# A second looped slot of one-hots in a graph kernel's matrix build, with the looped source one-hots made on ScalarE

## The reference

```
neigh = segment_sum(h1[src], dst, num_segments=N)              # layer 0
msg   = where(edge_type == 0, msgs[0], msgs[1]); agg = segment_sum(msg, row)   # layer 1, twice
agg   = segment_sum(h[src], dst); z = (1 + e) * h + agg        # layer 2, five times
out   = segment_sum(support[src] * edge_vals[:, None], dst)    # layer 3
```

## Time and profile before

| | us |
|---|---|
| median of three runs | 1826.44 |
| lowest and highest | 1819.98, 1828.72 |
| the profiled execution | 1818.69 |
| its span | 1816.4 |
| the build in it | about 20 to 316 |

### The profile page before, as it was taken

The page is one execution under the profiler, slowest core; times in us unless marked ns, Lnnn a source line. Parts: engine busy times, 40 slices in busy tenths (PEclk is TensorE's granted clock), DMA queues, the critical chain, the costliest instruction groups (busy, mean ns, idle before and its releaser), DMA issues.

```text
span 1816.4 us, 22290 instructions
## 1 busy us (share of the span) xinstructions
PE 1754.4 (97%) x7318; PEld 849.3 (47%) x7318; DVE 874.3 (48%) x1889; ACT 593.8 (33%) x1232; POOL 10.8 (1%) x36
## 2 busy tenths in 40 slices
PE   5989888999999999999999999999999999999998
PEld 3555555433334444444444444444544444444444
DVE  7888887489885321112222224334253443594123
ACT  1555544466876311222110001232323323232000
POOL 1000000000000000000000000000000000000000
PEclk9999999999999999999999999999999999999999
DMA  7999989810302401000011116300000010021111
GB/s 176 247 288 280 247 235 245 318 36 2 144 24 82 168 4 43 0 1 23 0 47 35 35 35 241 147 0 30 1 0 30 1 41 1 1 82 58 35 47 47
DMA packets 45781, 157.80 MB, mean 87 GB/s; under 512 B 7686, under 2 KB 9630, under 8 KB 37094
## 3 DMA queue, kind: packets, MB, share of 16 engines
q1 hardware_dynamic: 43792, 146.95, 26.6%
q10 hardware_dynamic: 1878, 9.44, 1.4%
HBM read 120.71 MB, written 35.65 MB: 86 GB/s over the span
## 4 chain that ended last, share of the span: by engine, by line
PE 83%; DVE 6%; DMA 5%; issue 3%; DVEq 2%; ACT 1%; POOL 0%; POOLq 0%; ACTq 0%
PE psum L1549 31%; PE psum L1563 31%; PE psum L1790 7%; DMA hs<-in_L_gnn_basis 4%; PE psum L1477 2%; PE psum L1444 2%; PE psum L1740 2%; PE psum L1637 2%; PE psum L1624 1%; PE psum L1476 1%; PE psum L1515 1%; DMA adj<-in_L_gnn_basis 1%; DVE hs L716 1%; DVEq L695 1%; PE psum L1716 1%
## 5 line engine op out<-in xcount | busy, mean ns | idle before, releaser
L1563 PE MATMUL psum<-hs,adj 128*128 128x512 f16 x2880 | 636.3, 380 | 0.0
L1549 PE MATMUL psum<-wb,xt 128*128 128x512 f32 x1056 | 457.7, 593 | 0.0
L1563 PEld LDWEIGHTS psum<-hs,adj 128*128 128x128 f16 x2880 | 281.2, 98 | 330.6 <-issue 11.0
L1549 PEld LDWEIGHTS psum<-wb,xt 128*128 128x128 f32 x1056 | 199.2, 190 | 244.8 <-issue 243.2
L1328 ACT ACTIVATE ua<-ua 128x512 f32<-128x512 f32 x60 | 37.8, 629 | 314.9 <-DVE ua L1106 181.2
L1102 DVE SCALAR_TENSOR_TENSOR vt<-psum,scl,xt 128x512 f32<-128x512 f32 x60 | 44.8, 746 | 192.7 <-PE psum L1563 192.7
L1037 DVE TENSOR_TENSOR vt<-psum,adj 128x512 f32<-128x512 f32 x24 | 16.6, 692 | 249.0 <-PE psum L1549 249.0
L1549 PE MATMUL psum<-adj,xt 128*128 128x512 f32 x288 | 130.1, 595 | 0.0
L1790 PE MATMUL psum<-hs,adj 128*128 128x512 f32 (+1 forms) x312 | 123.8, 560 | 0.0
L1477 PE MATMUL psum<-hs 128*128 128x192 f32 x404 | 99.7, 329 | 0.0
L1316 ACT ACTIVATE lnst<-lnst,bcol 128x1 f32<-128x1 f32 x24 | 7.1, 295 | 280.1 <-DVE lnst L1015 270.6
(11 more groups left out here) (249 smaller groups left out, 1741.5 us busy)
## 6 DMA issues: line engine op xcount, KB each, us to landing
hs<-in_L_gnn_basis SPq DMA_DIRECT2D x38, 960.0 KB, 12.9
adj<-in_L_gnn_basis SPq DMA_DIRECT2D x26, 960.0 KB, 14.5
aw_scratch<-xt ACTq DMA_DIRECT2D x12, 768.0 KB, 10.4
adj<-aw_scratch SPq DMA_DIRECT2D x1, 9216.0 KB, 36.8
x_scratch<-adj SPq DMA_DIRECT2D x24, 256.0 KB, 2.3
hs<-x_scratch SPq DMA_DIRECT2D x24, 256.0 KB, 2.6
ts_scratch<-adj SPq DMA_DIRECT2D x2, 2304.0 KB, 19.0
as_scratch<-adj SPq DMA_DIRECT2D x1, 4608.0 KB, 16.8
```

What stands on the lines that cost most here:

```text
L1549: x = pe.matmul(psum[:, bank, :], xt[:, i, k, :], w[:, k, :], start=first and k == 0, stop=last and k == 3)
L1563: x = pe.matmul(psum[:, i % 2 + (4 * half if own else 0), :], adj[:, m, j, P * i:P * i + P], hs[:, t, half, j, :], start=n == 1 or (own an ...
```

## The change

There are two looped slots, used by even and odd windows. The source one-hot of a looped tile is no longer made by VectorE but by ScalarE, in two instructions: `Abs(key - column)` into a scratch array `apart_t`, then `Relu(1 - that)` into the slot. ScalarE does this in `sources(w + 2)`, which stands at the end of its iteration of window w, behind the evictions and lots; `sources(0)` and `sources(1)` run ahead of the loop. For each looped tile of window w + 2 it waits until the slot is free, so a second looped tile of a window waits until TensorE has counted that window's first. TensorE waits for `onehot_ready` of the slot (VectorE's keys) and for the new `source_ready`. The running sum over the steps is made twice, over even and over odd windows, since each slot has counts of its own.

```
-SLOTS = 5
+SLOTS = 6
+        looped_t = sb("looped", [P, P + W * NT + W * NT], F32)
...
+        apart_t = rest[:, N + 256 + 2 * SLOT:N + 512 + 2 * SLOT].rearrange("p (t x) -> p t x", t=2)
+        onehots_at = [pairs[0][:, 0, :], ..., pairs[1][:, 1, :], looped, looped_t[:, :]]
-        LOOPED = SLOTS - 1
+        def looped_slot(w):
+            return 4 + w % 2
...
-            step(dve.tensor_tensor_scan(wrow[0:1, 2, :], wrow[0:1, 1, :], wrow[0:1, 1, :], 0.0, ALU.add, ALU.bypass))
+            by_turn = wrow[0:1, :, :].rearrange("p a (w t) -> p a t w", t=2)
+            for t in range(2):
+                x = dve.tensor_tensor_scan(by_turn[:, 2, t, :], by_turn[:, 1, t, :], by_turn[:, 1, t, :], 0.0, ALU.add, ALU.bypass)
+            step(x)
...
                 with dve.Fori(0, steps) as q:
-                    dve.wait_ge(onehot_free[LOOPED], before + q + 1)
+                    dve.wait_ge(onehot_free[looped_slot(w)], before + q + 1)
                     last = nc.s_assert_within(first + q + 2, 0, EC - 1, skip_runtime_bounds_check_because=why)
-                    source(LOOPED, last)
-                    keys(LOOPED, last, n, u)
+                    keys(looped_slot(w), last, n, u)
...
+            def sources(w):
+                first, steps, before = unpack(act.value_load(wrow_i[0:1, 0, w:w + 1], min_val=0, max_val=PACKED))
+                apart = apart_t[:, w % 2, :]
+                with act.Fori(0, steps) as q:
+                    t = nc.s_assert_within(first + q + 2, 0, EC - 1, skip_runtime_bounds_check_because="a tile of this stretch")
+                    act.wait_ge(onehot_free[looped_slot(w)], before + q + 1)
+                    act.activation(apart, iota_s[:, 0:P], ACT.Abs, bias=ecol[:, 0, bass.ds(t, 1)], scale=-1.0).then_inc(apart_ready[w % 2], 1)
+                    act.wait_ge(apart_ready[w % 2], before + q + 1)
+                    act.activation(onehot_s[looped_slot(w)], apart, ACT.Relu, bias=1.0, scale=-1.0).then_inc(source_ready[w % 2], 1)
+            act.wait_ge(c_ready, 7)
+            sources(0)
+            sources(1)
...
-                act.wait_ge(onehot_free[LOOPED], through + 1)
+                act.wait_ge(onehot_free[looped_slot(w)], through + 1)
...
                 for lot in by_window[w]:
                     side_lot(*lot)
+                if w + 2 < NW:
+                    sources(w + 2)
...
                 with pe.Fori(0, steps) as q:
-                    pe.wait_ge(onehot_ready[LOOPED], before + q + 1)
-                    counts(b, LOOPED, False)
+                    pe.wait_ge(onehot_ready[looped_slot(w)], before + q + 1)
+                    pe.wait_ge(source_ready[w % 2], before + q + 1)
+                    counts(b, looped_slot(w), False)
```

More of the change, by code:

```diff
@@ L209, in program @@
         pairs.append(rest[:, N + 256:N + 256 + 2 * SLOT].rearrange("p (k x) -> p k x", k=2))
-        onehots_at = [pairs[0][:, 0, :], pairs[0][:, 1, :], pairs[1][:, 0, :], pairs[1][:, 1, :], looped]
+        apart_t = rest[:, N + 256 + 2 * SLOT:N + 512 + 2 * SLOT].rearrange("p (t x) -> p t x", t=2)
+        onehots_at = [pairs[0][:, 0, :], pairs[0][:, 1, :], pairs[1][:, 0, :], pairs[1][:, 1, :], looped, looped_t[:, :]]
         onehot_s = [v[:, 0:P] for v in onehots_at]
@@ L238, in program @@
         onehot_free = [sem(f"onehot_free{k}") for k in range(SLOTS)]
+        apart_ready, source_ready = [[sem(f"{what}{t}") for t in range(2)] for what in ("apart_ready", "source_ready")]
         krel_ready = sem("krel_ready")
@@ L707, in sources @@
                                   ecol[:, 0, bass.ds(t, 2)].unsqueeze(2).broadcast_to([P, 2, P]), ALU.is_equal)
-            def source(k, t):
-                dve.tensor_scalar(onehot_s[k], iota_s[:, 0:P], ecol[:, 0, bass.ds(t, 1)], None, ALU.is_equal)
             def keys(k, t, n, u):
```

## The result

The change makes the kernel slower. The median is 1846.08 us (1844.25 to 1848.44, four runs) against 1823.21 us for the kernel before on the same chip (1814.05 to 1828.72, four runs): a ratio of 1.0132 [1.0112, 1.0152], some 24 us (the medians themselves lie 22.9 apart). The profiled execution after took 1848.44 us, against 1818.69 of the one before, so the two profiles lie 30 us apart, which is more than the medians do; single executions of the kernel before spread over 15 us.

The account below looks back on a forecast made before the run. The prediction took the build as paced by its transfers, TensorE and VectorE close behind. Terms -2 + 0.2 + 1 + 7 + 3 = 9.2, taken as 10 us, gave 1836 us against the median 1826.4; 8-in-10 range 1812 to 1862.

Parts of the forecast that it names:

- VectorE's source goes: Build: VectorE loses 30.3 us of busy time; taken as 0 in the middle, 2 us gained at the start.
- The pair: ScalarE, each of 106 looped tiles: Abs 384 ns and Relu 310 ns, together 0.69 us, unable to overlap.
- A window's extra: ScalarE, per window: pair plus exposed register work, 0.69 + 0.55 = 1.25 us, bounds 0.69 and 1.6.
- The ten waits: ScalarE at ten windows with two looped tiles: idle about 1.5 us each, bounds 0 and 2.8; 12 us in the middle.
- The sum of the middle: ScalarE, 47.5 to 262.3: 209.6 us of work plus 12 of waits, 221.6, 7 us over 214.8.
- The last stretch: Build from 262.3 on: two more waits each delay a chunk's reissue about 1.5 us, 3 us in all.
- TensorE's waits for its semaphore: TensorE, each looped tile: one more semaphore, 51 ns, 5.4 us if exposed, taken as hidden under matmuls: 0.
- the chain ahead of the build: Ahead of the build: one more running sum, under 0.35 us, overlapping the first, taken as 0.2 us.
- ScalarE far behind: Rival, middle: register work exposed in full, 1.6 us a window, 34 us over, 6 more at the ends: 1866; chance 0.08.
- VectorE was the brake: Rival, build: transfers have room, VectorE's keys hold TensorE; about -17 us, 1809; chance 0.17.
- The transfers keep the pace: Rival, build: ScalarE fits in, change does nothing that shows, between -8 and +4 us: 1824; chance 0.25.
- The rule weighed on the transfers: Basis chunk loads: by the 358 GB/s limit a chunk needs some 2.9 us; set aside for the trace's 216 GB/s.

Follow-up runs that it names:

- m_lean_wait: e_lean with all sources made two windows ahead again, so the ten waits are back; 1825.60 us, 1.0011 of the kernel before.
- i_one_load: Changed kernel with one ScalarE register load a window less, eviction's count kept from the value loaded for `sources`, ten waits kept; 1827.4 us, 1.0018 of before.
- c_free_source: Changed kernel in which nobody makes the looped tiles' sources, slots zeroed once, counts of looped tiles left out; 1817.9 us, 0.9965 of before.
- b_two_slots: Changed kernel with the looped sources back on VectorE, so the kernel before with a second looped slot alone; 1823.18 us, 0.9996 of before.
- e_lean: a_kept without the second register load a window on ScalarE, nothing else changed; 1822.8 us, 1.0009 of the kernel before.
- d_before_half: Kernel before with 60 of 120 partitions of every basis chunk loaded and used; 1822.2 us, 0.9993 of the kernel before.
- d_free_half: c_free_source with 60 of 120 partitions of every basis chunk loaded and used; 1809.1 us, 0.9931 of the kernel before.
- a_kept: Changed kernel with only the first looped tile's source made two windows ahead, later ones just ahead of their own window's eviction; 1843.84 us, 1.0110 of before.
- f_single: Changed kernel without the Abs and its register work, one Relu of the column numbers making each looped source; 1821.7 us, 0.9998 of before.
- h_one_ahead: Changed kernel with the sources made one window ahead in place of two; 1883.10 us, 1.0344 of the kernel before.

## Why the prediction was right, and where its sizes failed

The direction, the place and the mechanism were as forecast, and the time lies in the range; the size was not: 10 us forecast, 24 by the ratio and 30 between the profiles. Luck had two parts in it. The prediction named the wrong brake for the kernel before; that did no harm, as it charged ScalarE's work against the measured length of the middle, whatever set it. And its direction hung on the waits: ScalarE's work alone, 209.6 us, still fitted into 214.8. Measured, the work alone is already 217.2 (162.0 + 55.2), and m_lean_wait and i_one_load show that waits of the same size cost next to nothing where it is less. Point by point:

- **VectorE's source goes, 0 in the middle, 2 us at the start.** Nearly right by c_free_source (6 us in all), for a reason that was half wrong. The prediction had the transfers as the pace; halving them brought 1 us, some 6 with all of the clock's part allowed for. Its gain of 2 us at the start did not come: 22.0 us against 21.5.
- **The pair, 0.69 us.** 0.714 by the rows; right, no table load on top.
- **A window's extra, X = 1.25.** The first step that failed. In the middle ScalarE has 51.1 us more busy time and 55.2 us of issue gaps, which makes (51.1 + 55.2) / 79 = 1.35. Its parts are 0.65 for the pair (51.1 / 79; the two overlap their neighbours a little), 0.50 behind the Relu (39.7 / 79, forecast 0.55), and 0.20 ahead of the Abs (15.5 / 79), where the forecast took 0 as "hidden by the lot in front". It isn't hidden behind the DMA issue of L1181, which stood in the code and which the sum passed over: that write comes nine times in the middle, and at the six of them that an Abs follows at once, ScalarE stands 1.43 to 1.48 us, 8.7 of the 15.5 us. The other 6.8 us lie in 13 gaps of 0.4 to 0.7 us. The term was too small by 0.1 x 79, 7.5 us.
- **The ten waits, 1.5 us each.** 22.1 us in ten, 2.2 each; 17.4 in the middle where 12 was forecast: 5 us. Their places were right; the longest took 3.5, over the bound of 2.8.
- **The sum of the middle.** 221.6 forecast, 240.3 measured, 18.7 missing: 7.5 and 5.4 from the two terms above, 3.5 of small waits (2.1 + 1.4) and 2.2 that stand in no row. None of these is large. They count in full because the forecast's ScalarE already stood 7 us over the stretch: past that edge an error of 0.1 us a window is paid 79 times. i_one_load shows it from the other side, 21 us for one load a window.
- **The last stretch, +3.** Measured 56.7 against 53.7: +3.0.
- **TensorE's waits for its semaphore, the chain ahead of the build, the start.** The first eviction comes 0.2 us later and the start is 0.5 us longer, where 1.2 was forecast for chain and table load. b_two_slots has the longer chain and loses nothing; TensorE's added semaphore wait was not tried alone.
- **The clock** was taken as full throughout. It wasn't (below); TensorE is busy 5.7 us longer for the same matmuls. The profiled execution before, with 1.000, is not typical of its kernel either, which has 0.998 in the mean.

Of the rivals, "ScalarE far behind" (X = 1.6, 1866) had the better picture of what was to come, ScalarE past the edge, and too high an X. "VectorE was the brake" falls by c_free_source and by i_one_load and e_lean: where ScalarE keeps up the time is that of before, not 17 us less. "The transfers keep the pace" has the right time for the lean versions, 1823 to 1827; the runs don't bear out its reason.

The signs that were named came: L1214's wait for TensorE 9.9 us (under 50), ten waits before the Abs, TensorE waiting for ScalarE's turn copies, VectorE's busy time down (238.3 to 218.0 us in the build, 20 rather than 30), the DMA share at 0.91 in the middle. Of the two signs of being wrong, the pair with its register work under 1 us a window did not come (1.35). The other, chunk issues closer than 4.5 us, can't tell: they are 2.6 to 14.2 us apart before already, and on average 5.2 after instead of 4.68.

The rule weighed on the transfers (the Trainium skill, DMA: Bandwidth & Descriptors, section Bandwidth, about 358 GB/s) was set aside because "nowhere in the build is the traffic at that level, 261 GB/s with everything in it". That reading was wrong: 261 is a mean over 215 us, and the same trace has 350 GB/s over 10 us and 405 over 3 us in the build, all traffic taken together (shown at d_before_half). The kernel after has such a stretch too, 356 GB/s in 288.3 to 291.3 (last section). So the 216 GB/s of the earlier trace rows were what was asked for in that stretch, and not the most that the transfers can do, and d_before_half says the same. The rival that the prediction tied to the rule and calls the third is "VectorE was the brake", the second in its list. The rule's premise, transfers with time to spare, is borne out; the gain of 17 us is not, as even with sources that cost nobody anything (c_free_source) only 6 us came.

**What stays open.** The clock's exact part of the 24 us: a kernel with the same gaps but full clock was not tried. The mean granted clocks, 0.9960 after against 0.9980 to 0.9986 before, bound it by an estimate: (0.0020 to 0.0026) x 1846, 4 to 5 us at most. Whether i_one_load (1.0018) and m_lean_wait (1.0011), which keep the ten waits, still lose a little against e_lean (1.0009), which doesn't, is within their intervals. And that two brakes share the build before rests on d_free_half, whose interval allows a plain sum too, and on d_before_half, which was disturbed by its clock.

## What to carry to other kernels

Slack that an engine shows as one large wait (137 us here) is to be charged with everything that its queue has to run, in order: instructions, register loads, loop ends, DMA issues, and waits in front of work that others need. When the sum comes near the length of the stretch, the price per item turns from nothing to full, so the thing to look for is one item to leave out (here one register load a window, 21 us), not the wait that catches the eye. And a DMA share of 94% doesn't name the brake: look in the same trace for short stretches that move much more at that share (405 GB/s against 261 here), and then vary the bytes.

## What the runs showed of the hardware

**TensorE's clock in a busy build.** The profiled execution before had the full clock (1.00) all through the build. After, the granted clock fell to its lower level (1.2 GHz, half) four times for 3.4 us. The first two falls with what stood ahead of them, and what followed the first:

```profile
213.00:216.00 3.00, 0.65 (x3) 0.38 (x3) 2.84 (x9) 2.17 (x6) 0.00 (x0) 1.00 0.97 218
216.00:219.40 3.40, 3.11 (x16) 2.77 (x17) 2.62 (x10) 2.85 (x9) 0.00 (x0) 0.53 0.93 212
...
288.30:291.30 3.00, 0.88 (x5) 0.52 (x5) 2.61 (x10) 2.41 (x7) 0.00 (x0) 1.00 0.97 356
291.30:294.70 3.40, 3.40 (x19) 1.49 (x18) 3.05 (x9) 2.09 (x7) 0.00 (x0) 0.50 0.22 47
```

Ahead of these two TensorE was busy 0.65 and 0.88 of 3 us, each time with a wait of 1.5 to 2.1 us for ScalarE in it; ahead of the two later ones (305.0 and 328.9) 0.65 and 1.12, with such a wait too. Then it had a backlog, and worked it off at half speed. Four times 3.4 us at half speed are at most 6.8 us, and TensorE's busy time for the same 1793 matmuls rose by 5.7. In a_kept it rose by 9.3 and in d_before_half, where only the chunks and the matmuls over them got smaller, by 7.7. The measure itself scatters by some 4 us (e_lean shows 4.3 less than before), so these are sizes and no more. It is a cost that no list of waits shows. That the lull brings the fall isn't shown by these rows, only that it stood ahead of all four.

Such falls aren't the change's own. b_two_slots, c_free_source and i_one_load have two in their profiled builds and f_single four of 3.4 us, as many as after, and none of the four is slower than the kernel before by more than the noise. Nor does TensorE's idle time in the build put the kernels in order: d_before_half idles 28.1 us at a mean clock of 0.9953, a_kept 47.2 at 0.9908, h_one_ahead 87.2 at 0.9938. In d_before_half the chunk matmuls also contract 60 partitions in place of 120; whether that bears on the clock was not tried. Comparing the mean clocks of two kernels shows when a small difference in time may be the clock's.

**Where ScalarE is full, its register work is as dear as its arithmetic.** A window's second register load with its register operations (0.28 + 0.16 us) weighed as much as the Abs of 0.40 us: taking away either gave back 21 and 24 us.
